# Scattering routed rows from the left and from the right: both choices sent without a wait between them

## The chip, the cores and the metric

One core of one Trainium2 chip runs the whole program in one launch. The metric is the device time of an execution in microseconds (us). PE is TensorE, DVE is VectorE, ACT is ScalarE, POOL is GpSimd, SP is SyncE, which here only issues DMAs. All data are float32.

## The reference, cut to what matters

Two layers run one after the other on x of 4 batches x 1024 rows x 256 columns (4096 rows, 32 tiles of 128 rows). The change is in the feed-forward part of the first layer:

```python
shared = silu(X @ sW1 + sb1) @ sW2 + sb2
logits = einsum('btd,ed->bte', X, routing_W) + expert_bias
activation = sqrt(softplus(logits))
top_vals, top_idx = top_k(activation, 2)          # 2 of 8 experts, with their weights
combine = sum(one_hot(top_idx, 8) * top_vals[..., None], axis=-2)
hdn = silu(einsum('nd,edh->enh', Xf, rW1) + rb1)  # h = 128
y = einsum('enh,ehd->end', hdn, rW2) + rb2
routed = einsum('ne,end->nd', combine, y)
x = x + shared + routed                            # X is layernorm(x)
```

Before it stands a memory update (a strided convolution over 64 rows and a layer norm, added to x); after it a second layer with cross attention to 64 context rows and a feed-forward part of 8 experts with its own routing.

## The kernel before, in words

Each engine has one instruction list written out by hand; semaphores order them. The first layer's feed-forward is done in two groups of 16 tiles (`LG = 2`, `LT = 16`). For group g:

- `memory_norm`, `memory_add` and `scores` (DVE) make the normed rows in the tile `N0`, PE turns them and makes the router's logits, ACT copies them out (`l_lt` counts these copies, `l_xa` those of the turned rows).
- `choose(g)` (DVE) picks the two best experts of each row, gives each (row, choice) a place in a list sorted by expert (`slots`), and the two weights. Weight 1 is written into the column behind the row in `N0`, weight 2 into `m2`. Then it raises `rout`.
- `send_rows(g)` (POOL) scatters each tile of 128 rows twice into the DRAM tensor `XS`, once for each choice, with an indirect DMA of whole rows of `XW = 260` elements: 256 of data, the weight, and padding. 16 DMAs go out for the first choice. Then, for each half of the tiles: wait until that half has landed, copy weight 2 over weight 1 in `N0` (L560), drain, and send the half for the second choice. In group 1 the sends are broken every four tiles by waits on `f_ys`, the count of routed tiles done.
- `routed_rows(g)` (SP) waits for all 32 scatters, and loads the list back in 40 tiles of 128 slots (`LS = 40`) into the buffers `fx`, six tiles ahead.
- `routed(g)`: DVE reads the tile's expert number into a register (`value_load`) and copies that expert's first matrix (`fw1`, L1706); PE transposes the tile (L863), DVE copies it out (`fxT`, L1708), PE makes the hidden layer, ACT applies silu, PE makes the output, and ACT scales it by the weight that came along in the row (`scale`, L1248). SP stores it to `YL`, from where POOL gathers it by row (L571). In PE's order iteration j is `xpose(j + 2)`, `up(j + 1)`, `down(j)`; DVE's `fw1` of tile j needs the silu of tile j - 2.

The order of the work around the change on PE and ACT is: `fold` of the attention weights for pairs 3 to 7 (ACT's copies are counted by `st_sb`), `shared_up` for group 0 (its silus are counted by `l_hs`), `scores(1)`, `shared_down` for group 0 (its copies are L1218, counted by `l_ev`), then `routed(0)`, the shared part of group 1, `routed(1)`, a meeting of all engines, and the second layer. `routed(0)` on PE waits for `l_ev` of all four quads; on DVE it follows `choose(1)`. The second layer's own sends (L621) already carry the weights on both sides of the row.

Of the kernel before, what the change touches and what calls it, by code (L numbers as in the profile page):

```python
# [89 lines left out]
def build(nc, x, ctx_in, conv_w, conv_b, rout_w, rout_b, sw1, sb1, sw2, sb2, rw1, rb1, rw2, rb2,  # L90
          wq, bq, wk, bk, wv, bv, wo, bo, wr, w1, w2, w3, out):
    st = ExitStack()
    with st:
# [61 lines left out]
        wcol = sb("wcol", [P, 4])  # L155
# [17 lines left out]
        N0 = sb("N0", [P, TILES, XW], stack=s1)  # L173
# [26 lines left out]
        fx = [sb(f"fx{k}", [P, XW], stack=s2)[:, :] for k in range(XB)]  # L200
# [29 lines left out]
        def row_tile(m):  # L230
# [46 lines left out]
            l_sa l_sb l_sc2 l_nr l_tp l_xa l_xd l_lg l_lt l_tn l_ev l_su l_hs l_sy l_xu  # L277
# [43 lines left out]
        def _(sp):  # L321
# [7 lines left out]
            def memory_rows(b):  # L329

                t0, k = b * BT, S // RATE
                sp.dma_start(N0[:, t0:t0 + 4, 0:D],
                             x[b, k:k + CONV, :].rearrange("(t p) d -> p t d", p=P)).then_inc(s[f"s_in{b}"], 16)
                sp.dma_start(N0[:, t0 + 4:t0 + 7, 0:D],
                             x[b, CONV + S:T - S, :].rearrange("(t p) d -> p t d", p=P)).then_inc(s[f"s_in{b}"], 16)
                sp.dma_start(N0[0:S, t0 + 7, 0:D], x[b, T - S:T, :]).then_inc(s[f"s_in{b}"], 16)
                sp.dma_start(N0[S:P, t0 + 7, 0:D], ctx_in[b]).then_inc(s[f"s_in{b}"], 16)

# [106 lines left out]
            for sent in ("l_sa", "l_sb"):  # L445
                sp.wait_ge(s[sent], 8 * LT * LG + 16 * FREED)
# [27 lines left out]
        def _(po):  # L474
# [38 lines left out]
            po.memset(N0[:, :, D:XW], 0.0)  # L513
# [25 lines left out]
            def send(k, t0, t1, done, slot0=None):  # L539

                for t in range(t0, t1):
                    if slot0 is not None and (t - t0) % BREAK == 0 and slot0 + SLOTS * ((t - t0) // BREAK) > 0:
                        po.wait_ge(s["f_ys"], slot0 + SLOTS * ((t - t0) // BREAK))
                    po.indirect_dma_start(  # L544
                        XS, bass.IndirectOffsetOnAxis(ap=slot[k][:, t:t + 1], axis=0),
                        N0[:, t, :], None).then_inc(s[done], 16)

            def send_rows(g):
# [3 lines left out]
                half = LT // 2  # L552
                parts = [(LT * g, "l_sa"), (LT * g + half, "l_sb")]
                step = SLOTS * half // BREAK
                paced = [step * i + 2 - SLOTS if g else None for i in range(4)]
# [60 lines left out]
            def scatter(k, t0, t1):  # L616

                part = (slice(0, X0 + D), slice(X0, XW))[k]
                for t in range(t0, t1):
                    done = ("l_sa", "l_sb")[k] if t < FREED else f"sc{k + 1}"  # L620
# [59 lines left out]
        def _(pe):  # L680
# [173 lines left out]
            def routed(g):  # L854
# [3 lines left out]
                def xpose(j):  # L858
# [3 lines left out]
                    for c in range(DC):  # L862
                        last = nc.tensor.transpose(bank[j % 2][:, c * P:c * P + P], fx[j % XB][:, c * P:c * P + P], ident[:, :])  # L863
# [239 lines left out]
        def _(ac):  # L1103
# [130 lines left out]
            def routed(g):  # L1234
# [9 lines left out]
                def scale(j):  # L1244
# [3 lines left out]
                    act(fy[j % YB], bank[(7, 5)[j % 2]][:, 0:D], ACT.Copy, scale=fx[j % XB][:, D:D + 1]).then_inc(s["f_ys"], 1)  # L1248
# [208 lines left out]
        def _(ve):  # L1457
# [121 lines left out]
            def memory_add(g):  # L1579

                k = P - S // RATE
                for b in (2 * g, 2 * g + 1):
                    ve.wait_ge(s[f"x_in{b}"], 16)
                    for i in (0, 1, 2, 4, 5, 6, 7, 3):
                        t, n = b * BT + i, {3: k, 7: S}.get(i, P)
                        stt(X[0:n, t, :], N0[0:n, t, 0:D], rstd[0:n, t:t + 1], X[0:n, t, :], ALU.mult, ALU.add)
# [624 lines left out]
```

## Time and profile before

| | |
|---|---|
| median of 3 runs | 910.0 us (909.23 to 913.66) |
| the profiled execution's own time | 908.59 us |
| its span | 906.8 us |
| PE, DVE, ACT, POOL busy | 87%, 55%, 54%, 47% of the span |
| mean granted TensorE clock | 0.952 of full speed |
| group 0's scatters on POOL | 89.15 to 144.70 us |
| first routed tile of group 0 on PE | 149.06 us |
| last matmul of group 1's routed tiles | 301.17 us |

Times within the span are counted from its start. The span is the time from the first to the last instruction of the profiled execution; the execution's own time is 1.8 us longer. An engine's idle time is put down to what ended it; "issue" means that the profile shows nothing that the engine waited for.

### The profile page before, as it was taken

How to read it: one execution, taken by the hardware profiler on the slowest of the kernel's cores; microseconds unless marked ns; L12 is line 12 of the kernel's file. 1: busy time of each engine (PE TensorE's matmuls, PEld its weight loads, DVE VectorE, ACT ScalarE, POOL GpSimd, SP SyncE). 2: the span in 40 equal slices, each digit the busy share in tenths (PEclk: the TensorE clock that was granted, in tenths of full speed). 3: DMA queues.
4: the chain of work that ended last, by engine and by line, in shares of the span. 5: the costliest groups of instructions: out<-in, count | busy, mean ns of one | idle time of the engine just before them, and what ended most of it. 6: DMA issues, size and time to landing. Idle time of an engine off the chain costs nothing.

```text
span 906.8 us, 16543 instructions
## 1 busy us (share of the span) xinstructions
PE 786.6 (87%) x4538; PEld 682.2 (75%) x4538; DVE 497.1 (55%) x1345; ACT 488.6 (54%) x1374; POOL 430.0 (47%) x398
## 2 busy tenths in 40 slices
PE   2989986888999689999999998784789999999992
PEld 1646545776778479999989997774689999999991
DVE  5837945532455468888889888670122222244242
ACT  1357644534466378888777785351334444445441
POOL 2200735552786079888546778246642222222221
PEclk9799997989999789999999998997999999999997
DMA  8899984765699693464600514622322222255524
GB/s 254 278 314 313 318 286 136 241 193 168 143 234 238 221 266 82 71 167 85 172 1 1 188 70 141 193 65 99 106 95 71 66 67 70 81 193 182 187 90 160
DMA packets 122115, 143.02 MB, mean 158 GB/s; under 512 B 10391, under 2 KB 113612, under 8 KB 121004
## 3 DMA queue, kind: packets, MB, share of 16 engines
q1 hardware_dynamic: 90520, 92.03, 33.8%
q0 software_dynamic: 19856, 38.88, 15.8%
q10 hardware_dynamic: 11654, 11.05, 3.7%
q8 instruction: 44, 0.72, 0.3%
q14 instruction: 41, 0.34, 0.1%
HBM read 71.28 MB, written 70.65 MB: 157 GB/s over the span
## 4 chain that ended last, share of the span: by engine, by line
PE 67%; issue 8%; DVE 6%; ACT 5%; POOL 4%; DMA 4%; another core or an unknown queue 3%; DVEq 1%; SPq 1%; POOLq 0%; ACTq 0%
PE psum L684 24%; PE psum L960 8%; PE psum L982 8%; PE psum L1048 5%; PE psum L1053 5%; PE psum L1049 5%; POOL xs_dram L544 3%; PE psum L970 3%; PE psum L1062 2%; ACT pr L1330 2%; PE psum L863 2%; PE psum L1032 2%; DMA X<-in_x_dram 1%; DMA fx<-xs_dram 1%
## 5 line engine op out<-in xcount | busy, mean ns | idle before, releaser
L633 POOL DMA_INDIRECT yk_dram<-ys,L x71 | 70.3, 990 | 201.3 <-ACT ys L1402 198.7
L1048 PE MATMUL psum<-whi,xTh 128*128 x284 | 110.4, 389 | 23.3 <-ACT xTh L1384 16.5
L2113 DVE TENSOR_TENSOR hs<-psum,hs 128x384 f32<-128x384 f32 x71 | 39.7, 559 | 151.0 <-PE psum L1053 102.9
L544 POOL DMA_INDIRECT xs_dram<-N,slots x64 | 66.8, 1043 | 108.0 <-DVEq L1687 50.8
L571 POOL DMA_INDIRECT X<-yl_dram,slots_y x64 | 100.5, 1571 | 35.4 <-issue 14.8
L1330 ACT ACTIVATE pr<-psum,nmx 128x64 f32<-128x64 f32 x512 | 108.0, 362 | 15.1 <-DVE nmx L2019 14.9
L684 PE MATMUL psum<-w_sb,cz 128*128 x426 | 104.5, 381 | 2.2 <-ACT ys L1402 1.2
L1049 PE MATMUL psum<-wlo,xTh 128*128 x284 | 96.9, 341 | 0.0
L684 PEld LDWEIGHTS psum<-w_sb,cz 128*128 128x128 f32 x426 | 75.8, 191 | 10.7 <-issue 3.3
L1053 PE MATMUL psum<-whi,xTl 128*128 x284 | 75.3, 346 | 3.9 <-DVE xTl L2132 3.9
L621 POOL DMA_INDIRECT xs_dram<-N,slots x64 | 66.6, 1040 | 21.4 <-issue 18.0
L1048 PEld LDWEIGHTS psum<-whi,xTh 128*128 128x128 f32 x284 | 54.7, 193 | 27.9 <-issue 26.3
L613 POOL TENSOR_TENSOR pr<-pr,sm 128x1024 f32<-128x1024 f32 x32 | 62.5, 1952 | 25.9 <-DVE sm L2026 23.2
L1390 ACT ACTIVATE cz<-psum 128x384 f32<-128x384 f32 x69 | 33.8, 490 | 74.6 <-PE psum L1062 52.0
L684 PE MATMUL psum<-rw_sb,fh 128*128 x160 | 55.9, 432 | 10.9 <-issue 5.4
L1396 ACT ACTIVATE hs<-psum 128x384 f32<-128x384 f32 x71 | 34.9, 492 | 54.6 <-PE psum L1053 44.3
L1402 ACT ACTIVATE ys<-psum,wcol 128x256 f32<-128x256 f32 x71 | 33.6, 473 | 45.0 <-PE psum L684 38.7
L1248 ACT ACTIVATE fy<-psum,fx 128x256 f32<-128x256 f32 x80 | 37.9, 473 | 34.1 <-PE psum L684 24.9
L1053 PEld LDWEIGHTS psum<-whi,xTl 128*128 128x128 f32 x284 | 52.2, 193 | 5.2 <-DVE xTl L2132 5.2
L1049 PEld LDWEIGHTS psum<-wlo,xTh 128*128 128x128 f32 x284 | 54.9, 193 | 1.6
L684 PE MATMUL psum<-fxT,fw 128*128 128x128 f32 x320 | 52.4, 289 | 4.0 <-DVE fxT L1708 1.9
L684 PE MATMUL psum<-b2p,ones 128*128 (+1 forms) x112 | 53.7, 479 | 0.0
(338 smaller groups left out, 1871.2 us busy)
## 6 DMA issues: line engine op xcount, KB each, us to landing
fx<-xs_dram SPq DMA_DIRECT2D x80, 130.0 KB
xs_dram<-fill SPq DMA_DIRECT2D x4, 2600.0 KB
yl_dram<-fy SPq DMA_DIRECT2D x80, 128.0 KB
xs<-xs_dram SPq DMA_DIRECT2D x71, 130.0 KB
wlo<-in_L_ffn_W_dram SPq DMA_DIRECT2D x4, 1536.0 KB, 7.0
ym<-yk_dram ACTq DMA_DIRECT2D x12, 512.0 KB
xs_dram<-cz SPq DMA_DIRECT2D x1, 5200.0 KB, 27.0
xs_dram<-cz SPq DMA_DIRECT2D x8, 650.0 KB
```

The lines of the kernel that those rows point to most:

```text
L544: po.indirect_dma_start(XS, bass.IndirectOffsetOnAxis(ap=slot[k][:, t:t + 1], axis=0), N0[:, t, :], None).then_inc(s[done], 16)
L571: po.indirect_dma_start(X[:, t, :], None, YL[b // 2], bass.IndirectOffsetOnAxis(ap=slot_y[k][:, t:t + 1], axis=0), compute_op=ALU.add).the ...
L613: po.tensor_tensor(v, v, sm[n % 2][:, :].rearrange("p (a b) -> p a b", b=1).to_broadcast([P, NHEAD, S]), ALU.mult).then_inc(s["a_pn"], 1)
L621: po.indirect_dma_start(XS1, bass.IndirectOffsetOnAxis(ap=slot[k][:, t:t + 1], axis=0), row_tile(t)[:, part], None).then_inc(s[done], 16)
L633: po.indirect_dma_start(YK, bass.IndirectOffsetOnAxis(ap=yid[:, j:j + 1], axis=0), ys[j % YB], None).then_inc(s[f"y_out{j % YB}"], 16)
L684: return nc.tensor.matmul(o, l, r, start=start, stop=stop)
L960: last = nc.tensor.matmul(bank[2 * b + h], a[b][:, c, :], w[k][:, c, cols_], start=i == c == 0, stop=i == 2 and c == DC - 1)
L982: last = nc.tensor.matmul(bank[7][:, 0:D], a[:, c * P:c * P + P], w[k][:, c, :], start=i == c == 0, stop=i == 2 and c == PAIRS - 1)
L1048: nc.tensor.matmul(o, xTh[b][:, c, :], wh[c], start=c == 0, stop=False)
L1049: nc.tensor.matmul(o, xTh[b][:, c, :], wl[c], start=False, stop=False)
L1053: last = nc.tensor.matmul(o, xTl[b][:, c, :], wh[c], start=False, stop=c == DC - 1)
L1330: last = act(pr[b][:, S * h:S * h + S], bank[2 * b + h // 8][:, S * (h % 8):S * (h % 8) + S], ACT.Exp, bias=nmx[:, h:h + 1])
```

## The change

- The row in `N0` is moved two elements to the right (`X0 = 2`): weight 1 stands in element 1, left of the data, and weight 2 in element 258, right of it. The first choice scatters elements 0 to 257, the second elements 2 to 259, into `XS` seen as single elements; `slots` therefore counts elements, in two `tensor_scalar` where there was one.
- With both weights in place, no row is rewritten between the choices. The waits for landing, the copies of weight 2 and the drains go.
- Where a choice doesn't write, the slot keeps the zero it was cleared to, so the weight of a slot is the sum of elements 1 and 258. DVE makes this sum for four tiles at a time into `wcol`, in each `j % 4 == 1`, with waits for the loads of the next two tiles and a drain behind it; ACT's `scale` reads `wcol` and waits for it in each `j % 4 == 0`.
- In group 0 the 32 scatters are broken by four waits: before number 8 for `st_sb`, 14 for `l_hs`, 20 for `l_xa`, 26 for `l_lt`. In group 1 the waits on `f_ys` stand at the same numbers as before.
- The semaphores `l_sa`, `l_sb`, `l_sc2` become `l_s0` and `l_s1`, one for each group.

```diff
-        wcol = sb("wcol", [P, 4])
+        wcol = sb("wcol", [P, XB])
...
-        N0 = sb("N0", [P, TILES, XW], stack=s1)
+        N0w = sb("N0", [P, TILES, XW], stack=s1)
+        N0 = N0w[:, :, X0:X0 + D]
...
-                for done in ("l_sa", "l_sb"):
-                    sp.wait_ge(s[done], 8 * LT * (g + 1))
-                sp.wait_ge(s["l_sc2"], 16 * LT * (g + 1))
+                sp.wait_ge(s[f"l_s{g}"], 16 * 2 * LT)
...
-            po.memset(N0[:, :, D:XW], 0.0)
+            po.memset(N0w[:, :, 0:X0], 0.0)
+            po.memset(N0w[:, :, X0 + D:XW], 0.0)
...
-                for (t, done), at_slot in zip(parts, paced):
-                    send(0, t, t + half, done, at_slot)
-                for (t, done), at_slot in zip(parts, paced[2:]):
-                    po.wait_ge(s[done], 16 * half * (g + 1))
-                    po.tensor_copy(N0[:, t:t + half, D:D + 1], m2[:, t:t + half].rearrange("p (t a) -> p t a", a=1))
-                    po.drain()
-                    send(1, t, t + half, "l_sc2", at_slot)
+                for i in range(2 * LT):
+                    k, t = i // LT, LT * g + i % LT
+                    if g and i and i % BREAK == 0:
+                        po.wait_ge(s["f_ys"], SLOTS * (i // BREAK) + 2 - SLOTS)
+                    if g == 0 and i == 8:
+                        po.wait_ge(s["st_sb"], 4 * PAIRS - 3)
+                    if g == 0 and i == 14:
+                        po.wait_ge(s["l_hs"], 2)
+                    if g == 0 and i == 20:
+                        po.wait_ge(s["l_xa"], LQ + 3)
+                    if g == 0 and i == 26:
+                        po.wait_ge(s["l_lt"], 2 * LQ)
+                    part = (slice(0, X0 + D), slice(X0, XW))[k]
+                    po.indirect_dma_start(
+                        XS1, bass.IndirectOffsetOnAxis(ap=slot[k][:, t:t + 1], axis=0),
+                        N0w[:, t, part], None).then_inc(s[f"l_s{g}"], 16)
...
-                    act(fy[j % YB], bank[(7, 5)[j % 2]][:, 0:D], ACT.Copy, scale=fx[j % XB][:, D:D + 1]).then_inc(s["f_ys"], 1)
+                    if j % 4 == 0:
+                        ac.wait_ge(s["f_xt"], j + 3)
+                    act(fy[j % YB], bank[(7, 5)[j % 2]][:, 0:D], ACT.Copy, scale=wcol[:, j % XB:j % XB + 1]).then_inc(s["f_ys"], 1)
...
-                ts(slots[:, :, t0:t0 + n], hot2[:, :, 0:n], float(base), None, ALU.add)
+                for k in range(2):
+                    ts(slots[:, k, t0:t0 + n], hot2[:, k, 0:n], float(XW), float(XW * base + X0 * k), ALU.mult, ALU.add)
...
-                tt(N0[:, t0:t0 + n, D], sp_x[:, 0, :], sp_r[:, 0, :], ALU.mult)
-                tt(m2[:, t0:t0 + n], sp_x[:, 1, :], sp_r[:, 1, :], ALU.mult)
+                tt(N0w[:, t0:t0 + n, X0 - 1], sp_x[:, 0, :], sp_r[:, 0, :], ALU.mult)
+                tt(N0w[:, t0:t0 + n, X0 + D], sp_x[:, 1, :], sp_r[:, 1, :], ALU.mult)
...
+                    if j % 4 == 1:
+                        k = j % XB - 1
+                        for i in (1, 2):
+                            ve.wait_ge(s[f"xs_in{(j + i) % XB}"], 16 * ((j + i) // XB + 1))
+                        if j > XB:
+                            ve.wait_ge(s["f_ys"], j - 5)
+                        tt(wcol[:, k:k + 4], fx8[:, k:k + 4, X0 - 1], fx8[:, k:k + 4, X0 + D], ALU.add)
+                        ve.drain()
```

## Rows read from the trace of the kernel before

**Rows 1.** The page's costliest groups; columns as in the page: busy, mean ns, idle before.

```profile
L544 POOL DMA_INDIRECT xs_dram<-N,slots x64 | 66.8, 1043 | 108.0 <-DVEq L1687 50.8
L621 POOL DMA_INDIRECT xs_dram<-N,slots x64 | 66.6, 1040 | 21.4 <-issue 18.0
```

**Rows 2.** The chain that ended last, 100 to 160 us: start, us, what.

```profile
111.51 6.75 issue
...
128.39 6.48 issue
...
143.74 2.25 DMA xs_dram<-N,slots
...
149.06 1.08 PE psum L863 x4
150.23 1.22 PE psum L684 x4
```

**Rows 3.** POOL in order of time: its DMAs and what follows a drain.

```profile
28.10 0.91 POOL L508 DMA_DIRECT2D wo_sb<-in_L_xattn_Wo_dram  x1
...
37.93 0.11 POOL L527 MEMSET segm<- 128x8 f32 x1 [5.93 <-issue]
...
128.17 0.21 POOL L560 COPY N<-m 128x8 f32<-128x8 f32 x1
```

**Rows 4.** The DMA issues: KB each, median us to landing.

```profile
wo_sb<-in_L_xattn_Wo_dram POOLq DMA_DIRECT2D x1, 1024.0 KB, 9.6
```

**Rows 5.** ACT in order of time, 100 to 145 us.

```profile
102.01 0.60 ACT L1175 ACTIVATE st_r<-psum 128x512 f32<-128x512 f32 x1 [0.26 <-issue]
...
108.98 0.69 ACT L1208 ACTIVATE cu<-psum,cols 128x512 f32<-128x512 f32 x1 [1.03 <-issue]
...
119.38 0.60 ACT L1191 ACTIVATE xT<-psum 128x512 f32<-128x512 f32 x1 [0.43 <-issue]
...
126.96 0.59 ACT L1185 ACTIVATE convw_sb<-psum 8x512 f32<-8x512 f32 x1 [2.01 <-PE psum L684]
...
141.92 1.08 ACT L1218 ACTIVATE ysh<-psum 128x512 f32<-128x512 f32 x2 [2.61 <-PE psum L684]
```

**Rows 6.** DVE in order of time: the end of choose(1) and the first routed tile.

```profile
140.36 0.18 DVE L1653 TENSOR_SCALAR slots<-hot 128x32 int32<-128x32 f32 x1
140.45 0.17 DVE L1654 CAST slots_y<-hot 128x32 int32<-128x32 f32 x1
...
144.28 0.40 DVE L1700 COPY rw_sb<-cols 128x8 f32<-128x8 f32 x1
145.75 0.31 DVE L1706 COPY fw<-rw_sb 128x257 f32 x1 [1.07 <-issue]
149.75 0.42 DVE L1708 COPY fxT<-psum 128x256 f32<-128x256 f32 x1 [3.69 <-issue]
```

**Rows 7.** DVE in order of time, one shared_add, one halt, a quick stretch.

```profile
164.96 1.22 DVE L1694 TENSOR_TENSOR X<-X,wq_sb 128x1024 f32<-128x1024 f32 x1
166.09 0.29 DVE L1706 COPY fw<-rw_sb 128x257 f32 x1
...
194.02 0.30 DVE L1706 COPY fw<-rw_sb 128x257 f32 x1 [2.94 <-issue]
...
199.94 0.42 DVE L1708 COPY fxT<-psum 128x256 f32<-128x256 f32 x1
200.90 0.30 DVE L1706 COPY fw<-rw_sb 128x257 f32 x1 [0.53 <-issue]
201.16 0.43 DVE L1708 COPY fxT<-psum 128x256 f32<-128x256 f32 x1
```

**Rows 8.** PE in order of time, the same quick stretch.

```profile
200.96 0.61 PE L684 MATMUL psum<-fxT,fw 128*128 128x128 f32 x4
...
202.18 0.61 PE L684 MATMUL psum<-fxT,fw 128*128 128x128 f32 x4
```

**Rows 9.** PE by windows of 2 us: busy (count), granted clock, DMA share, GB/s.

```profile
144.00:146.00 2.00, 0.00 (x0) 0.61 0.37 133
```

More of the change, by code:

```diff
@@ L199, in build @@
         sb("under_slots", [P, 2 * HK + TILES * XW + 3 * DC * NHEAD * DH], stack=s2)
-        fx = [sb(f"fx{k}", [P, XW], stack=s2)[:, :] for k in range(XB)]
+        fx8 = sb("fx8", [P, XB, XW], stack=s2)
+        fx = [fx8[:, k, :] for k in range(XB)]
         fxT = [sb(f"fxT{k}", [P, DC, P], stack=s2)[:, :, :] for k in range(2)]
@@ L331, in memory_rows @@
                 t0, k = b * BT, S // RATE
-                sp.dma_start(N0[:, t0:t0 + 4, 0:D],
+                sp.dma_start(N0[:, t0:t0 + 4, :],
                              x[b, k:k + CONV, :].rearrange("(t p) d -> p t d", p=P)).then_inc(s[f"s_in{b}"], 16)
-                sp.dma_start(N0[:, t0 + 4:t0 + 7, 0:D],
+                sp.dma_start(N0[:, t0 + 4:t0 + 7, :],
                              x[b, CONV + S:T - S, :].rearrange("(t p) d -> p t d", p=P)).then_inc(s[f"s_in{b}"], 16)
-                sp.dma_start(N0[0:S, t0 + 7, 0:D], x[b, T - S:T, :]).then_inc(s[f"s_in{b}"], 16)
-                sp.dma_start(N0[S:P, t0 + 7, 0:D], ctx_in[b]).then_inc(s[f"s_in{b}"], 16)
+                sp.dma_start(N0[0:S, t0 + 7, :], x[b, T - S:T, :]).then_inc(s[f"s_in{b}"], 16)
+                sp.dma_start(N0[S:P, t0 + 7, :], ctx_in[b]).then_inc(s[f"s_in{b}"], 16)
             def x_rows(b):
@@ L443, in _ @@
             weights(2)
-            for sent in ("l_sa", "l_sb"):
-                sp.wait_ge(s[sent], 8 * LT * LG + 16 * FREED)
+            sp.wait_ge(s["l_s1"], 16 * 2 * (LT + FREED))
             weights(3)
@@ L537, in after @@
                     po.wait_ge(s[other], n)
[L539 to L546, printed above, removed]
             def send_rows(g):
@@ L551, in send_rows @@
                 po.wait_ge(s["rout"], g + 1)
[L552 to L555, printed above, removed]
-                for (t, done), at_slot in zip(parts, paced):
-                    send(0, t, t + half, done, at_slot)
-                for (t, done), at_slot in zip(parts, paced[2:]):
-                    po.wait_ge(s[done], 16 * half * (g + 1))
-                    po.tensor_copy(N0[:, t:t + half, D:D + 1], m2[:, t:t + half].rearrange("p (t a) -> p t a", a=1))
-                    po.drain()
-                    send(1, t, t + half, "l_sc2", at_slot)
+                for i in range(2 * LT):
[14 more added lines that the diff above has]
+                        N0w[:, t, part], None).then_inc(s[f"l_s{g}"], 16)
             def collect(b, k, t0, t1):
@@ L619, in scatter @@
                 for t in range(t0, t1):
-                    done = ("l_sa", "l_sb")[k] if t < FREED else f"sc{k + 1}"
+                    done = "l_s1" if t < FREED else f"sc{k + 1}"
                     po.indirect_dma_start(
@@ L862, in xpose @@
                     for c in range(DC):
-                        last = nc.tensor.transpose(bank[j % 2][:, c * P:c * P + P], fx[j % XB][:, c * P:c * P + P], ident[:, :])
+                        last = nc.tensor.transpose(bank[j % 2][:, c * P:c * P + P], fx[j % XB][:, X0 + c * P:X0 + c * P + P], ident[:, :])
                     last.then_inc(s["f_tp"], 1)
@@ L1601, in rows_in @@
                     for t in range(QT * q, QT * q + QT):
-                        last = ts(N0[:, t, 0:D], X[:, t, :], mean[:, t:t + 1], rstd[:, t:t + 1], ALU.subtract, ALU.mult)
+                        last = ts(N0[:, t, :], X[:, t, :], mean[:, t:t + 1], rstd[:, t:t + 1], ALU.subtract, ALU.mult)
                     last.then_inc(s["l_nr"], 1)
```

6 lines of the change are left out of this document (3 added, 3 removed).

## The prediction

> **What bounds the kernel now.** I read the page first: PE is busy 87% of the span, so most of the program is PE work, and POOL's scatter L544 appears high among the groups with 64 instructions and 66.8 us [rows 1]. A share of the span doesn't say whether a scatter costs time, so I went to the chain of work that ended last and looked at 100 to 160 us. There the chain isn't on PE: it runs through group 0's scatters on POOL, through two gaps of 6.75 and 6.48 us before the 17th and the 25th scatter, then a landing of 2.25 us, the load of a tile, and only then PE's first routed tile at 149.06 and its first hidden layer at 150.23 [rows 2]. That is the stretch that the change touches. To see what would be late next I read ACT, DVE and PE in order of time around it [rows 5 to 8], and the granted clock there [rows 9].
>
> **What the two gaps are.** Each gap stands behind a copy of weight 2 (the second copy at 128.17 [rows 3]), not before it, so when the copy ran the half that it rewrites had landed, and what took 6.5 us was the drain. POOL's other drain behind DMAs looks the same: the last weight load is issued at 28.10, takes 9.6 us to land [rows 4], which is 37.7, and POOL goes on at 37.93 after 5.93 us of idle time [rows 3]. So a drain on POOL seems to last until what POOL has sent has landed. The change removes the copies (0.2 us each) and these drains: 6.75 + 6.48 + 0.4 = 13.6 us off POOL's own line.
>
> **What the four waits give back.** One scatter follows another by 1.27 us (0.96 us and 0.30 us of issue, the pitch in the undisturbed runs of them). The eighth started at 100.13.
> - Number 8 (counted from 0) would start at 101.4; it waits for the copy that ACT starts at 102.01 and ends at 102.61 [rows 5], and with 0.3 us of release starts at 102.9.
> - Number 14 would start six pitches later, 110.5; its silu ended at 109.67 [rows 5], so it waits for nothing.
> - Number 20: 118.1, but the turned rows that it waits for are out at 119.98 [rows 5], so 120.3.
> - Number 26: 127.9; the logits that it waits for are out at 127.55 [rows 5], nothing.
> - Number 31, the last: 127.9 + 5 x 1.27 = 134.2, against 143.74 before.
>
> So the scatters end 9.5 us sooner; 4 us of the 13.6 go to the waits. The loads would be there 9.5 us sooner too, which puts PE's first transpose at 139.5 as far as data go.
>
> **What is late next.** PE can't start `routed(0)` before ACT's last shared copy, which ends at 143.0 [rows 5]; that is still no limit, because DVE comes later. It has `choose(1)` to finish, then the bias copy at 144.28, and `fw1` of the first tile at 145.75 [rows 6]. In the kernel before `fw1` was already there and `fxT` waited for the tile until 149.75. After the change the tile waits for DVE. Where nothing holds it up, `fxT` starts 0.26 us behind `fw1` (200.90 and 201.16 [rows 7]). To this come the split `slots` instruction: the start-to-start step of such a small one is 0.09 us [rows 6], once in each `choose`, both on DVE's line to this point, 0.18 us. So `fxT` starts at 145.75 + 0.18 + 0.26 = 146.19 instead of 149.75. **The gain at the start of routed(0) is 3.6 us, not 9.5 and not 13.6.** This line has a cushion for the scatters: their landing may take up to 142.4 (146.2 less the 3.1 us from landing, 145.99, to the first transpose, and the 0.7 us from there to `fxT` [rows 2, 6]), 7 us after the last one is issued. Landing took 2.25 us when the DMA engines had little to do [rows 2], about 6.5 us in the busier time behind each drain. Both fit. If the cushion were used up, each us over it is a us of the gain.
>
> **What the weight sums cost.** There are 20 of them, with a drain each, on DVE. The trace has no such operation; it has two neighbours. One is the bias copy, also with a drain behind it and a register load next: `fw1` starts 1.07 us after the copy's end [rows 6]. Applied to a sum of 0.17 us that starts 0.34 us behind the start of `fxT`, it puts the next `fw1` 1.58 us behind `fxT`. In the quick stretch it starts 0.96 us behind (199.94 to 200.90), and the next `fxT` 0.26 us after it [rows 7]. That is 0.62 us later for DVE. The low end is 0.11 us: 0.59 us until the drain is through, and 0.48 us for the register load (no less than 0.56 us from `fxT` start to `fw1` start is seen anywhere, less the step of issue). PE needs the copy that started at 201.16 only for the hidden layer at 202.18, and the copy ends at 201.59 [rows 7, 8]: 0.6 us of slack. The other neighbour is `shared_add`: it occupies DVE for 1.22 us and `fw1` starts 1.13 us after it, 1.48 us behind `fxT` [rows 7], and PE's period around it isn't visibly longer than elsewhere in this stage, while the quick stretch has 1.22 us [rows 8]. With 0.62 us more against 0.6 us of slack and 0.1 us from the copy's end to PE's start, one sum costs between 0 and 0.12 us of PE's time in the quick stretch, and nothing in the slower ones. I take 0.05 us, as the sums lie nearest to `shared_add`: 20 x 0.05 = 1.0 us, bounds 0 and 20 x 0.12 = 2.4 us. Without PE's slack it would be 20 x 0.62 = 12.4 us.
>
> The DVE row says that a drain with a register load behind it has a price of 1.07 us [rows 6]. The Trainium skill ("VectorE: DVE Perf Modes", section "The DRAIN you can't avoid") says that every DVE instruction has its pipeline flush anyway and that adding synchronization costs nothing extra. By that the drains would be free, the sums only 0.17 us each, and the total for them 0 instead of 1.0 us. Only the instruction behind it is counted there, not a register load; the row here is the dearer one and the sum goes by it.
>
> **Costed at nothing.** ACT's wait in `j % 4 == 0` needs `fxT` of tile j + 2. That copy follows its transposes, which PE does before `up(j + 1)` and `down(j)`; in the quick stretch it ends 0.5 us before the output that ACT scales is made, 0 if the sum takes the full 0.62 us; silu of the next tile stands behind it and has a tile of slack. DVE's waits for the loads of the next two tiles: the loads run six tiles ahead, and PE waits for tile j + 2 before `up(j + 1)` anyway; behind DVE's wait stand `fw1` and `fxT`, which PE wants at the same moment. Scaling by `wcol` instead of `fx`: the same instruction. The second memset of POOL stands before the drain that waits for a landing until 37.9 [rows 3], so its 0.15 us is covered; uncovered it would be just that. Scatter of 258 instead of 260 elements: the second layer's L621 does this at 1040 ns against 1043 ns [rows 1]. Group 1's scatters: their copies and drains go too, but the last batch still hangs on `f_ys` 32, and POOL isn't on the chain there. Its first four stay where they are, behind `rout` at about 144.4.
>
> **The sum.** -3.6 + 1.0 = -2.6 us. The span goes from 906.8 to 904.2 and the profiled execution's own time from 908.59 to 906.0. The median of the runs shown was 910.0, 1.4 us above that execution, so I forecast 907.4. From `routed(0)` on everything hangs on PE and moves along with it: POOL's gathers start on the stores of group 0, the meeting of the engines on the last tile of group 1.
>
> **Rivals.**
> - *More comes back than the start.* PE stood idle from 142 to 149, its granted clock fell (0.61 in the mean of 144 to 146 [rows 9]) to the lower of its two levels, 1.2 GHz. Now four transposes can run at 143.1, and PE is idle for 3 us instead of 7. The first hidden layer took 1.22 us there and takes 0.61 us at the full clock [rows 2, 8]. If the clock stays up, the first two save 0.6 us each, 1.2 us together, and the rest of those tiles stands beside other waits. The Trainium skill ("TensorE: Matmul & The Clock Gate", Part 1) has the lower level as the default and activity as what lifts it; by that rule the transposes may or may not do, so it gives 906.2 or 907.4. Also, in `routed(0)` the engines stood still before 194.02, DVE for 2.94 us with nothing to wait for [rows 7], just after POOL had sent eight scatters without a break, the first four of them late by the drain. If spreading them cures this: 907.4 - 2.9 = 904.5, and with both 903.3. Against: nothing in the profile ties the halt to the scatters. Chance 0.27.
> - *The weight sums are not covered.* Slower than before: DVE's 0.62 us shows on PE at each of 20 places, 910.0 - 3.6 + 12.4 = 918.8. It eats the gain from 0.18 us for each sum on, and is slower by over 0.5% from 0.41 us on. For it: the DVE line of `fw1`, `fxT`, `up`, silu is a loop of its own, near PE's pace. Against: `shared_add` of 1.22 us leaves no such mark. Chance 0.12.
> - *The scatters land late.* Their last six now go out at 128 to 135, while the expert weights are loaded. If landing takes 10 us or more, the start hardly moves: 910.0 - 0.5 + 1.0 = 910.5. Chance 0.08.
> - *The whole shift of 9.5 us counts.* Only if `choose(1)` came earlier too, which nothing in the change does: 901.5. Chance 0.03.
> - My forecast, 905.2 to 909.2: 0.50.
>
> **How the numbers follow.** 0.5% is 4.55 us, about what a measurement of this kernel can tell from no change; faster means under 905.45, slower over 914.55. Faster: 0.8 of the first rival (0.22), the fourth (0.03), and 0.07 of my own case: 0.32. Slower: most of the second rival, 0.10. The same: 0.58. The range reaches to the first rival's 903.3 less 0.8 us and up past the third's 910.5 by the top of the sums' bound: 902.5 to 912. Left out are the fourth rival, the dear end of the second and the tails.
>
> **What the profile after would show.** Right: no gap over 3 us in POOL's group 0 scatters except 1.3 us before number 8 and 2 us before number 20; the last one starts near 134; `fx` loads near 138; PE transposes two tiles near 143.2, then waits for DVE; the first `fxT` at about 146.2. The period of PE in `routed(0)` and `routed(1)` unchanged outside the halts, 20 additions of under 0.2 us. Wrong: `fxT` of the first tile waits for a load, or `routed(1)` ends less than 2 us earlier than 301.2 with the start 3.6 us earlier (the sums cost), or the halts of `routed(0)` are shorter or longer by more than 2 us, which would outweigh both terms.

## The result and the profile after

The changed kernel takes 928.81 us (median of 4 runs, 926.69 to 929.46) against 909.62 us (4 runs): ratio 1.0222 [1.0178, 1.0265]. It is slower by 2.2%, well clear of the noise. (Ratios compare executions in the chip's fast state alone, medians are of all executions, so the two need not divide exactly.) The forecast was 907.4 us with a range up to 912. The profiled execution has a span of 924.9 us, 18.1 us longer than before's.

The page's groups for the two sends, to compare with [rows 1]: a scatter is as quick as before, and POOL's idle time ahead of the first layer's went up from 108.0 to 125.2 us.

```profile
L556 POOL DMA_INDIRECT xs_dram<-N,slots x64 | 64.4, 1006 | 125.2 <-DVEq L1686 68.7
...
L617 POOL DMA_INDIRECT xs_dram<-N,slots x64 | 65.8, 1029 | 21.3 <-issue 18.0
```

I followed the same stretch first: the chain of work that ended last, 84 to 165 us. Columns as in [rows 2].

```profile
113.02 7.48 another core or an unknown queue
120.52 0.70 DVE xT L1607
...
134.53 10.20 another core or an unknown queue
144.75 1.09 ACT wq_sb L1214 x2
...
161.82 0.23 DVE fxT L1707
162.09 0.71 PE psum L680 x4
```

The scatters and the two gaps of [rows 2] are off the chain, as forecast. In their place stand two pieces of 7.48 and 10.20 us for which the profile names no instruction. The first routed tile's hidden layer starts at 162.09 instead of 150.23 [rows 2]. The same two places, engine by engine in order of time (POOL's first four rows; then DVE, ACT, PE):

```profile
98.26 1.28 POOL L556 DMA_INDIRECT xs_dram<-N,slots  x1 [0.31 <-issue]
103.33 0.97 POOL L556 DMA_INDIRECT xs_dram<-N,slots  x1 [3.79 <-ACT st_r L1171]
...
117.34 0.97 POOL L556 DMA_INDIRECT xs_dram<-N,slots  x1 [0.30 <-issue]
127.67 0.96 POOL L556 DMA_INDIRECT xs_dram<-N,slots  x1 [9.36 <-ACT xT L1187]
...
141.75 0.97 POOL L556 DMA_INDIRECT xs_dram<-N,slots  x1 [0.30 <-issue]
```

```profile
120.52 0.69 DVE L1607 COPY xT<-psum 128x512 f32<-128x512 f32 x1 [7.50 <-remote]
```

```profile
120.52 1.08 ACT L1187 ACTIVATE xT<-psum 128x512 f32<-128x512 f32 x2 [5.54 <-remote]
144.75 1.08 ACT L1214 ACTIVATE wq_sb<-psum 128x512 f32<-128x512 f32 x2 [10.22 <-remote]
```

```profile
121.36 3.57 PE L680 MATMUL psum<-xT,cols 128*8 128x512 f32 x4 [5.87 <-DVE xT L1607]
145.98 1.19 PE L680 MATMUL psum<-sw_sb,cu 128*128 128x256 f32 x2 [8.60 <-ACT wq_sb L1214]
```

"Remote" means that the engine started when a semaphore rose, but that the profile found no instruction ending close enough to have raised it. I call such a place a halt.

The trace's record of semaphores tells whose signal it was: PE's. At the first place both engines wait for the semaphore of the transposes of L776, at the second ACT waits for that of the shared output matmuls. PE in order of time, and DVE's last instruction of its part of `choose(1)`:

```profile
113.52 1.97 PE L776 MATMUL psum<-ident,N 128*128 128x128 f32 x16 [0.78 <-issue]
...
136.91 0.47 PE L680 MATMUL psum<-b2p,ones 128*128 128x256 f32 x1
```

```profile
140.20 0.19 DVE L1674 TENSOR_TENSOR sp_x<-sp_x,m 128x32 f32<-128x32 f32 x1
```

The transposes are recorded as ended at 115.49 (113.52 + 1.97), and their semaphore rises at 120.50, 5.0 us later. The matmuls end at 137.38 (136.91 + 0.47), and theirs rises at 144.73, 7.35 us later. ACT and DVE start 0.02 us behind the rise each time, the same PE rows as in e4 are there without a gap, and DVE works on inside the second halt until 140.39. So a halt is a late signal of PE's, and part of the idle time in front of it (2.5 of DVE's 7.5 us, 2.85 of ACT's 10.2 us) is an ordinary wait for PE's work. Whether the matmuls themselves finished late (the profile models the ends of PE's work) or only their signals came late, the trace doesn't tell.

Now to when the signals come. POOL's scatters 8 to 19 end at 118.31 (117.34 + 0.97), and DVE and ACT come back 2.21 us later. Scatters 20 to 31 end at 142.72, and ACT comes back 2.03 us later. Of the four waits, two break nothing: numbers 14 and 26 follow without a gap, so POOL issues 12 scatters in a row, twice.

The stage behind it is longer as well. Times of `fxT`, first tile to last of each group (`routed(0)` is tiles 0 to 39, `routed(1)` 40 to 79), from DVE in order of time:

| | first scatter to first fxT | routed(0) | routed(1) | last fxT to the end |
|---|---|---|---|---|
| before | 60.6 | 69.3 | 58.8 | 608.4 |
| after | 73.0 | 69.3 | 64.9 | 608.3 |

So 12.4 us are lost ahead of the first routed tile and 6.1 us in `routed(1)`, and nothing elsewhere: 18.5 us, and the span is 18.1 us longer. In `routed(1)` each `fxT` after a weight sum comes late: the mean step from tile j to j + 1 is 2.66 us for j % 4 == 1, against 1.64 us before; the other three steps together are 0.4 us shorter. One such place, DVE, ACT, PE, SP in order of time:

```profile
266.58 0.43 SPq L398 DMA_DIRECT2D fx<-xs_dram  x1
...
271.57 0.42 DVE L1707 COPY fxT<-psum 128x256 f32<-128x256 f32 x1
...
272.01 0.37 ACT L1238 ACTIVATE fh<-psum,fw 128x128 f32<-128x128 f32 x1 [0.19 <-PE psum L680]
...
273.14 0.17 DVE L1714 TENSOR_TENSOR wcol<-fx 128x4 f32<-128x4 f32 x1 [1.15 <-DMA fx<-xs_dram]
...
273.78 0.38 PE L859 MATMUL psum<-ident,fx 128*128 128x128 f32 x2
274.28 0.30 DVE L1705 COPY fw<-rw_sb 128x257 f32 x1 [0.98 <-ACT fh L1238]
274.49 0.42 DVE L1707 COPY fxT<-psum 128x256 f32<-128x256 f32 x1
274.96 0.71 PE L680 MATMUL psum<-fxT,fw 128*128 128x128 f32 x4 [0.80 <-DVE fxT L1707]
275.02 0.47 ACT L1246 ACTIVATE fy<-psum,wcol 128x256 f32<-128x256 f32 x1 [1.26 <-DVE fxT L1707]
```

This is tile 53. DVE wants the load of tile 55, which SP had issued at 266.58 (counted by the stores between), and waits 1.15 us for it. PE transposes tile 55 only at 273.78, so the load came in time for PE. Then come the sum, the drain and the register load, and `fw1` of tile 54 starts 1.14 us after the sum. Its silu had ended at 272.38 (272.01 + 0.37); the wait put down to it was long over. PE idles 0.80 us and ACT 1.26 us. And since ACT's `scale` now waits for `fxT`, the count `f_ys` by which SP loads further tiles is held up too.

### The profile page after: what moved, and what is told of

The parts are those of the page before. It is cut to its first block, busy times and chain, and to the rows that moved or that the text cites. A ratio compares the mean times of both kernels' runs of the same rounds, so it can differ in the third digit from the quotient of the medians.

```text
span 924.9 us, 16596 instructions
## 1 busy us (share of the span) xinstructions
PE 789.5 (85%) x4538; PEld 681.1 (74%) x4538; DVE 500.4 (54%) x1367; ACT 487.8 (53%) x1374; POOL 423.6 (46%) x395
## 4 chain that ended last, share of the span: by engine, by line
PE 56%; DVE 11%; issue 8%; another core or an unknown queue 5%; POOL 5%; DMA 5%; ACT 4%; DVEq 4%; SPq 2%; POOLq 0%; ACTq 0%
PE psum L680 21%; PE psum L956 6%; PE psum L1044 5%; PE psum L978 5%; PE psum L1049 5%; PE psum L1045 5%; DMA fx<-xs_dram 3%; PE psum L1058 2%; POOL xs_dram L617 2%; PE psum L966 2%; PE psum L1028 2%; POOL pr L609 2%; ACT pr L1328 1%; DMA X<-in_x_dram 1%
## 5 line engine op out<-in xcount | busy, mean ns | idle before, releaser
L629 POOL DMA_INDIRECT yk_dram<-ys,L x71 | 69.5, 979 | 202.2 <-ACT ys L1400 200.4
L556 POOL DMA_INDIRECT xs_dram<-N,slots x64 | 64.4, 1006 | 125.2 <-DVEq L1686 68.7
L567 POOL DMA_INDIRECT X<-yl_dram,slots_y x64 | 100.0, 1563 | 33.6 <-issue 14.8
L1328 ACT ACTIVATE pr<-psum,nmx 128x64 f32<-128x64 f32 x512 | 108.0, 362 | 11.8 <-DVE nmx L2026 11.5
L617 POOL DMA_INDIRECT xs_dram<-N,slots x64 | 65.8, 1029 | 21.3 <-issue 18.0
L680 PE MATMUL psum<-fxT,fw 128*128 128x128 f32 x320 | 52.3, 288 | 10.1 <-DVE fxT L1707 8.6
L1246 ACT ACTIVATE fy<-psum,wcol 128x256 f32<-128x256 f32 x80 | 37.8, 473 | 40.4 <-PE psum L680 21.3
```

The costliest lines, as they stand in the source:

```text
L556: po.indirect_dma_start(XS1, bass.IndirectOffsetOnAxis(ap=slot[k][:, t:t + 1], axis=0), N0w[:, t, part], None).then_inc(s[f"l_s{g}"], 16)
L567: po.indirect_dma_start(X[:, t, :], None, YL[b // 2], bass.IndirectOffsetOnAxis(ap=slot_y[k][:, t:t + 1], axis=0), compute_op=ALU.add).the ...
L617: po.indirect_dma_start(XS1, bass.IndirectOffsetOnAxis(ap=slot[k][:, t:t + 1], axis=0), row_tile(t)[:, part], None).then_inc(s[done], 16)
L629: po.indirect_dma_start(YK, bass.IndirectOffsetOnAxis(ap=yid[:, j:j + 1], axis=0), ys[j % YB], None).then_inc(s[f"y_out{j % YB}"], 16)
L680: return nc.tensor.matmul(o, l, r, start=start, stop=stop)
L1328: last = act(pr[b][:, S * h:S * h + S], bank[2 * b + h // 8][:, S * (h % 8):S * (h % 8) + S], ACT.Exp, bias=nmx[:, h:h + 1])
```

## The experiments

Theory A: the engines halt because their next instructions don't come while POOL issues scatters without a pause; the drains before were the pauses. (What PE's late signals say of theory A stands under "What ends a halt".) Theory B: the weight sums cost the time. Theory C: the bulk transfers (expert weights, clearing) halt the engines whatever POOL does. Each call ran on one chip, with the kernel before beside it, and the chips turned out to differ: the kernel before takes 902 to 910 us on some and 866 to 868 us on others. Ratios are therefore always to before on the same chip.

**First call: group 0's breaks (before 867.62 us).** The four waits are replaced by before's drains, by nothing, or by short memsets; e4 keeps them and breaks group 1's scatters at every second one.

```diff
 e1_drains:   if g == 0 and i in (16, 24): po.drain()
 e2_one_run:  (nothing)
 e3_gaps:     if g == 0 and i and i % 4 == 0: three po.memset(scratch), each with a semaphore
 e4_pairs:    if g and i >= 4 and i % 2 == 0:
                  po.wait_ge(s["f_ys"], SLOTS * i // BREAK + 2 - SLOTS)
```

> The changed kernel with the four waits of group 0 replaced by a POOL drain before scatters 16 and 24; the weights stay on both sides, the weight sums stay. Theory A (an engine that needs its next instructions gets them only when POOL pauses between scatters, and the two halts of 7.5 and 10.2 us come from two unbroken runs of 12): the drains pause POOL for 6 to 7 us near 110 and 127 as in the kernel before, no halt over 3 us in 100 to 150 us, time 905 to 912. Rival B (the weight sums and their waits cost the 19 us): nothing changes there, 926 to 931. Rival C (the halts come from bulk transfers that fill the DMA engines, whatever POOL does): halts stay, 920 to 930.

> The changed kernel with no wait at all within group 0's 32 scatters: one run from 88.6 to about 129.3. Theory A: ACT and DVE, who want instructions near 113, halt until 1.5 to 2.2 us after the run's end, 131; then nothing is in the way of choose(1); first routed tile at 159 to 162, 920 to 930. Rival B: the scatters end earlier, 926 to 931 all the same, but without a halt at 131. Rival C: halts of the same length as in the changed kernel at about the same times, 926 to 931.

> The changed kernel with the four waits replaced by a short pause of POOL before every fourth scatter of group 0: three small memsets, each waited for by its semaphore (about 1 to 1.5 us). Theory A, if a pause of 1 us is enough: no run longer than 4 scatters, halts under 4 us, time 902 to 910. If the pause must be longer: one run until about 138, 930 to 940. Rival B: 926 to 931. Rival C: 920 to 931.

> The changed kernel with group 1's scatters broken after every second one instead of every fourth (waits on f_ys at even numbers, same average pace); group 0 as it is. Theory A: the two halts of group 0 stay, the halts in routed(0) (ends at 198.4, 209.1, 219.5, 228.2) shrink by 1 to 2 us each, 920 to 926. Rivals B and C: as the changed kernel, 926 to 931.

Measured: e1 882.05 us, 1.0171 [1.0108, 1.0233]; e2 874.89, 1.0095 [1.0056, 1.0133]; e3 871.67, 1.0054 [1.0023, 1.0085]; e4 873.71, 1.0069 [1.0039, 1.0098]. Theory A had the drains among the best; they are the worst. None of the four traces has a single halt, not even e2 with 32 scatters in a row. On this chip theory A has nothing to explain, and yet all four are slower than before. What they share is the weight sums.

**Second call: the sums (before 907.88 us).** e5 and e6 are the two kernels unchanged. e7 leaves the sums out, so that the rows of the second choice get weight 0; e8 makes them one tile at a time behind `fxT`, of a tile that has been transposed and so is there:

```diff
-                    if j % 4 == 1:
-                        ... (waits for two loads and f_ys)
-                        tt(wcol[:, k:k + 4], fx8[:, k:k + 4, X0 - 1], fx8[:, k:k + 4, X0 + D], ALU.add)
-                        ve.drain()
+                    tt(wcol[:, j % XB:j % XB + 1], fx[j % XB][:, X0 - 1:X0], fx[j % XB][:, X0 + D:X0 + D + 1], ALU.add).then_inc(s["f_w"], 1)
...
-                    if j % 4 == 0:
-                        ac.wait_ge(s["f_xt"], j + 3)
+                    ac.wait_ge(s["f_w"], j + 1)
```

> The kernel before, unchanged, so that its trace is there from the same chip as the others. Theory A (the engines halt while POOL scatters in long runs): its routed(0) takes longer than routed(1) by the halts, as in the first trace (69.3 us against 58.8 us from the first to the last fxT). Theory B (the weight sums cost the time): whatever the halts do, routed(1) takes 58 to 59 us, and the kernels with sums take about 6 us longer there (64 to 66 us).

> The changed kernel, unchanged. Theory A: ratio to before 1.015 to 1.03 wherever the halts show in the trace, and near 1.00 where they don't. Theory B: 10 to 13 us for the 20 sums, less 3 to 9 us that the start of routed(0) gains: ratio 1.003 to 1.01 without halts, and routed(1) 6 us longer than before's.

> The changed kernel without the 20 weight sums, their waits and their drains; ACT scales by the element on the left alone, so the second choice's rows get weight 0 (that part of the computation is left out). Theory B: 10 to 13 us under the changed kernel on the same chip, ratio to before 0.990 or less, routed(1) at 58 to 59 us. Theory A: the same time as the changed kernel within 3 us. My prediction's term: 1.0 us (0 to 2.4).

> The changed kernel with the weight summed tile by tile on DVE, right behind fxT, with a semaphore of its own and with neither a drain nor a wait for the loads of later tiles. Theory B in the form that the drain and the wait for loads cost the time, not the addition: within 3 us of the kernel without sums, ratio to before about 0.99. If the addition itself costs it: 80 x 0.15 us = 12 us over the kernel without sums. Theory A: no difference to the changed kernel.

Measured: e5 912.32 us in its one execution. e6 922.57, 1.0205 [1.0143, 1.0267]. e7 913.42, 1.0117 [1.0057, 1.0177]. e8 912.97, 1.0107 [1.0045, 1.0169]. The sums as the change makes them cost 9.2 us here (922.57 - 913.42, six executions each); made tile by tile, 80 additions in place of 20, they cost nothing measurable. So it isn't the addition (0.15 us each, in DVE's idle time) but what stands around it. With the sums gone the kernel is still slower than before by 1.2% [0.6%, 1.8%], and the stretch ahead of the first routed tile, with its halts, is what is left to differ (70.3 us against 60.2 in e5). They stand in e6, e7 and e8 at the same two places as in the first trace. e6, ACT in order of time:

```profile
117.97 1.08 ACT L1187 ACTIVATE xT<-psum 128x512 f32<-128x512 f32 x2 [5.29 <-remote]
...
141.38 1.08 ACT L1214 ACTIVATE wq_sb<-psum 128x512 f32<-128x512 f32 x2 [10.21 <-remote]
```

**Third call: the sums tile by tile, and group 0 in four ways (before 868.37 us).** e9 has the drains of e1, e10 the gaps of e3, e12 one run as e2, and e11 twelve memsets (3 us) before each of scatters 8, 16 and 24. All have e8's sums.

> Weights summed tile by tile, and in group 0 two drains on POOL (before scatters 16 and 24, where the kernel before has them) instead of the four waits. Theory A: where the halts exist, the stretch from the first scatter to the first fxT is that of the kernel before, 60 to 61 us, instead of 70 to 73 us; together with free sums the ratio to before is 0.995 to 1.003. Theory C (the DMA engines are full, whatever POOL does): the stretch stays at 70 us and the ratio at 1.01. On a chip without halts the drains keep the stretch at 61 us instead of 54 us: ratio 1.00.

> Weights summed tile by tile; group 0 in runs of four scatters with 0.8 us of memsets between them, instead of the four waits. Theory A: if 0.8 us lets a refill through, the halts are at most 5 us each, the stretch to the first fxT is 56 to 62 us, ratio 0.99 to 1.00; if a pause has to be longer than the 1.5 to 2.2 us by which the engines come back after a run, it is 70 us or more, as with one run. Theory C: 70 us. Without halts: 54 us, ratio 0.992.

> Weights summed tile by tile; group 0 in four runs of eight scatters with 3 us of memsets between them, instead of the four waits. Theory A: pauses are longer than the time in which the engines come back, so the halts shrink to what is left of a run: stretch 56 to 62 us, ratio 0.99 to 1.00. Theory C: 70 us, 1.01. Without halts: 54 us, ratio 0.992.

> Weights summed tile by tile; group 0's 32 scatters in one run of 41 us with no pause. Theory A: an engine that runs out of instructions behind the first scatters stands until 1.5 to 2.2 us after the run, so one halt of 15 to 19 us that ends 43 to 44 us after the first scatter, and the first fxT about 74 us after it; ratio 1.01 to 1.015. Theory C: halts at the same times as in the changed kernel, whether POOL's run goes on or not. Without halts: 54 us, ratio 0.992.

Measured: e9 868.03 us, 1.0007 [0.9977, 1.0037]; e10 863.23, 0.9939 [0.9915, 0.9962]; e11 862.66, 0.9940 [0.9907, 0.9973]; e12 862.25, 0.9939 [0.9915, 0.9963]. Again no halts, so A and C stay untested. But the parts come out clean. With the drains kept, the new layout of the rows costs and brings nothing (e9 = before). Taking the drains away brings 5.8 us (e9 to e12). How POOL is paced makes no difference. e12, DVE in order of time at the end of `choose(1)`:

```profile
142.07 0.17 DVE L1690 COPY rw_sb<-cols 128x8 f32<-128x8 f32 x1
143.32 0.49 DVE L1696 COPY fw<-rw_sb 128x257 f32 x1 [1.08 <-issue]
143.73 0.40 DVE L1698 COPY fxT<-psum 128x256 f32<-128x256 f32 x1
```

The tile is there, and `fxT` follows `fw1` by 0.41 us: DVE's own line sets the start, as forecast. With one run POOL's first scatter starts at 89.52 and `fxT` 54.21 us later. It is 54.20 to 54.22 us in all eight traces without halts of kernels that have neither drains nor pauses of 3 us, e4 with its four waits included; with the 3 us pauses it is 55.7 to 56.1 us.

**Further draws of a chip.** The kernels of e12 and e11 again, to meet a chip with halts; at last the changed kernel once more. (e13 to e16 ran on one and the same chip.)

> The same kernel as the one with one run of 32 scatters, for a chip on which the halts exist (before at about 909 us). Theory A: a halt of 15 to 19 us that ends 1.5 to 2.2 us after the run (43 to 44 us after the first scatter), first fxT about 74 us after the first scatter, ratio 1.01 to 1.015. Theory C: halts of 6 to 7 us and 10 us at the places of the changed kernel, 70 us. On a chip without halts (before at about 868 us): 54 us, ratio 0.994, as measured.

> The same kernel as the one with four runs of eight scatters and 3 us of memsets between them, for a chip on which the halts exist. Theory A: halts end within the pauses, so none is longer than 7 us and they sum to less than in the changed kernel: first fxT 56 to 62 us after the first scatter, ratio 0.99 to 1.00. Theory C: 70 us, 1.01. Without halts: 54 to 56 us, 0.994.

> One run of 32 scatters, weights tile by tile, in search of a chip on which the halts exist. Theory A there: first fxT about 74 us after the first scatter, the last halt ending 43 to 44 us after it, ratio 1.01 to 1.015. Theory C: 70 us, the halts at the places of the changed kernel. Without halts: 54 us, 0.991 to 0.994.

> Four runs of eight with 3 us of memsets between them, weights tile by tile, same chip as the run of 32. Theory A where halts exist: first fxT 56 to 62 us after the first scatter, ratio 0.99 to 1.00, no halt over 7 us. Theory C: 70 us, 1.01. Without halts: 54 to 56 us, 0.994 to 0.996.

> One run of 32 scatters, weights tile by tile, a further draw of a chip. Theory A where halts exist: the last halt ends 43 to 44 us after the first scatter and the first fxT is about 74 us after it. Theory C: first fxT at 70 us, halts where the changed kernel has them, the first ending 32 us after the first scatter. Without halts: 54 us, ratio 0.991 to 0.995.

> The changed kernel, unchanged, on a further draw of a chip. If the halts don't exist there (before at about 867 us), the stretch from the first scatter to the first fxT is 54 to 55 us as in the kernels with one run, and the sums cost 11 to 13 us over the kernels that sum tile by tile (which stand at 0.991 to 0.997): ratio 1.005 to 1.010. If they exist (before at about 908 us), the stretch is 70 to 73 us and the ratio 1.015 to 1.025, as on the two chips before. The theory that the halts alone make the change slow expects 0.99 on a chip without them.

Measured: one run 0.9914 [0.9881, 0.9947], 0.9949 [0.9913, 0.9985] and 0.9932 [0.9883, 0.9980] (e13, e15, e17); runs of eight 0.9964 [0.9929, 1.0] and 0.9976 [0.9928, 1.0024] (e14, e16), before at 865.7 to 867.9 us each time and no halts. Only e18 met a chip with halts, with the wrong kernel for the question: 922.44 us against 902.35, 1.0210 [1.0174, 1.0246]. It repeats the first result, with halts of 6.35 and 10.18 us.

**What separates the chips.** Times in us; the halts are those of over 1.3 us put down to "remote" ahead of the first routed tile:

| kernel (before on its chip) | halts | first scatter to first fxT | first to last fxT | last fxT to the end |
|---|---|---|---|---|
| before, first trace (909.6) | 6.5 | 60.6 | 148.7 | 608.4 |
| e5, before (907.9) | 2.3, 1.5, 4.1 | 60.2 | 147.9 | 609.0 |
| after, first trace (909.6) | 7.5, 10.2 | 73.0 | 155.0 | 608.3 |
| e6, after (907.9) | 6.4, 10.2 | 70.5 | 153.5 | 608.2 |
| e18, after (902.4) | 6.4, 10.2 | 69.9 | 150.5 | 609.2 |
| e7, no sums (907.9) | 6.7, 10.1 | 70.3 | 145.4 | 607.6 |
| e8, sums by tile (907.9) | 6.4, 9.4 | 71.5 | 142.9 | 607.3 |
| e1, drains (867.6) | none | 61.5 | 148.3 | 581.0 |
| e9, drains, by tile (868.4) | none | 60.3 | 135.9 | 581.2 |
| e2, one run (867.6) | none | 54.2 | 145.2 | 580.9 |
| e12, one run, by tile (868.4) | none | 54.2 | 136.1 | 579.5 |

The last column belongs to code that the change doesn't touch, and differs by 27 us between the chips. Most of it is the end of the stretch in which POOL sends the second layer's scatters and those behind them (L617 and L629): from 290 to 380 us behind the last `fxT` PE idles 24.3 us in after and 3.1 us in e12, and 66.7 against 43.3 us in the whole column. PE by windows, after and then e12: busy (count), other engines, granted clock, DMA share, GB/s.

```profile
600.00:700.00 100.00, 75.37 (x399) 69.11 (x398) 33.50 (x127) 35.09 (x90) 51.42 (x57) 0.90 0.27 88
```

```profile
600.00:700.00 100.00, 100.00 (x582) 95.16 (x581) 26.88 (x77) 48.33 (x128) 48.81 (x51) 1.00 0.34 103
```

In after DVE stands in that stretch for up to 12.8 us with "remote"; in e12 no engine does. The DMA share is 0.27 and 0.34: no shortage of DMA engines.

**What ends a halt.** In the five traces with the change's waits and with halts, POOL's second run of scatters ends between 115.90 and 122.48 us and the third between 139.35 and 145.50; the engines come back behind them by:

| | after | e6 | e7 | e8 | e18 |
|---|---|---|---|---|---|
| behind scatter 19 | 2.21 | 2.07 | 2.03 | 2.02 | 2.00 |
| behind scatter 31 | 2.03 | 2.03 | 1.94 | 1.21 | 1.99 |

In the first trace of before, where the run ends elsewhere, DVE's halt of 6.54 us ends at 129.82, 1.64 us behind the end of its run of eight (128.18). Against it stands one halt of e5, 2.27 us, that ended at 110.80 inside a run that went on to 114.66. So ends of long halts follow ends of POOL's runs, closely; that the one causes the other was not tested, as the kernels with longer and with shorter runs met no chip with halts.

The semaphores of all 20 traces carry it further. In the 13 traces without halts no signal of PE's, of some 890 in each, rises more than 0.015 us behind the recorded end of the work that raises it. In the seven with halts 245 rise over 1 us behind it. All of these lie inside a run of three or more of POOL's scatters (in the second layer also those of the outputs, L629) or at most 2.7 us behind one. None lies beside the 64 gathers (L567), which are indirect DMAs as well. The longest delay grows with the length of the run, by and large: 3.3 us for runs of four scatters, 6.1 us for eight, 7.35 us for twelve and 13.1 us for fourteen, but only 2.0 us for before's run of sixteen. This speaks for the half of theory A that ties the halts to runs of scatters. Counting in traces isn't an experiment, though: the runs differ in other ways too, and where a matmul's record is missing a single delay is less than it seems.

Against theory C: the second halt of after lies in 134.5 to 144.8, where the DMA share is 0.33 in both windows that hold it, on the same core that shows 1.02 in 88 to 98 us without a halt over 1.3 us. These are `after`'s windows:

```profile
88.00:98.00 10.00, 10.00 (x40) 7.43 (x40) 8.77 (x35) 7.08 (x14) 7.51 (x7) 1.00 1.02 325
...
132.00:142.00 10.00, 5.04 (x26) 2.89 (x25) 4.38 (x15) 0.97 (x2) 7.57 (x9) 0.91 0.33 116
142.00:146.00 4.00, 0.02 (x1) 0.05 (x1) 0.00 (x0) 1.08 (x2) 0.72 (x1) 0.50 0.33 110
```

The other half of theory A is that a halted engine is out of instructions. The page of after lists two queues for instructions:

```profile
q8 instruction: 44, 0.72, 0.3%
q14 instruction: 41, 0.34, 0.1%
```

The Trainium skill ("Runtime: NRT & Kernel Launch", section "Instruction fetch mechanics") says that instructions are fetched in blocks of 16 KiB over a DMA queue of their own, and that this is mostly hidden. For q8 the size agrees (0.72 MB in 44 packets), q14's packets are half as large. That a late fetch makes the halts is what the trace speaks against. ACT and DVE weren't out of instructions, as they started 0.02 us behind PE's signal. And the second halt goes by without a fetch: these are all the queues that moved anything in after from 123 to 152 us, and none is one for instructions.

```profile
q1 hardware_dynamic: 3749, 3.81, 41.4%
q0 software_dynamic: 576, 1.59, 15.2%
```

The second halts of e6, e7, e8 and e18 have no such packet either. Inside the first halt of after one packet starts, at 115.55, and it is over at 116.49, 4.0 us before the signal. What holds PE's signals back stays open.

## Why the prediction was wrong

- **The two gaps are drains that wait for landing: right.** With drains in place of the waits the gaps are back at their places (9.04 and 6.62 us in e1, 8.26 and 6.32 us in e9, against 6.75 and 6.48 us [rows 2]).
- **The four waits give back 4 us, last scatter at 134.2: wrong, and without weight where there are no halts.** Number 20 went at 127.67 instead of 120.3, as the turned rows that it waits for came out behind the first halt. In e4, without halts, scatter 31 starts 43.8 us after the first (forecast 134.2 - 89.15 = 45.05) and the start of `routed(0)` is that of one run.
- **The gain at the start, 3.6 us: this step failed.** Its mechanism is right (DVE's `choose(1)` and `fw1` come last; 54.21 us in e12), and without halts it brings 6.1 us (e9 to e12, 60.27 to 54.21). But the term took DVE's line from the trace before as fixed: `fxT` at 146.19, 57.0 us behind the first scatter. That line hangs on PE's signals. Without late ones it takes 54.2 us, so those of the trace before had put 2.8 us into it. In the changed kernel it takes 73.0 us, and e4, with the same group 0 on a chip without halts, 54.2: the halts cost 18.8 us there, and the start came 11.9 us later instead of 3.6 us earlier. Before had halts as well and lost nothing by them at the start (60.6 and 60.2 us with halts, 60.3 us in e9 with drains and without halts), because POOL's line with its drains ended last and covered them. The change took the cover away, and the halts grew: ahead of the first tile the longest delay of a signal is 1.8 and 2.0 us in the two traces of before and 7.35 us in after. That the cover is gone and that they grew is shown by these numbers, why they grew isn't. I had seen one halt [rows 7], and counted its cure as a possible gain, with the remark that nothing tied it to the scatters. The mirror of it, that the change makes them longer, stands in the prediction only as a sign of being wrong, for `routed(0)`, and was no rival with a price.
- **The weight sums, 1.0 us (0 to 2.4): this step failed too.** They cost 9.2 us by the medians of e6 and e7, and 9 to 12 us between e2 and e12 or e1 and e9 by the time from the first to the last `fxT` (145.2 to 136.1, 148.3 to 135.9). The second rival had this at 12.4 us, with a chance of 0.12. Two entries under "costed at nothing" were wrong. "The loads run six tiles ahead": they are issued six tiles ahead, but for tile 55 it took 6.5 us from the issue to the start of the sum, and DVE, whose line is ahead of PE's, asks for them earlier than PE does; it idled for them 11 times, 13.6 us, in e1. And ACT's wait for `fxT` of tile j + 2 had slack only as long as that copy isn't late: it waited 7.8 us in seven places (150 to 300 us of after). How much is the drain with the register load and how much the early wait wasn't separated: e8 takes both away. The low price rested on a gap of 1.58 us from `fxT` to the next `fw1`. At tile 53 it was 2.71 us (271.57 to 274.28), as the wait for the load came on top. (That no step from `fxT` to `fw1` is under 0.56 us doesn't hold either: one is 0.33 us in the trace before, 242.26 to 242.59. The figure went only into the low end.)
- **The slack of 0.6 us on PE [rows 7, 8] and `shared_add` as a neighbour** were the reason for the low price. The slack is real in a quick stretch, but the sum doesn't come there: it waits for loads, which `shared_add` doesn't.
- **The sum.** -3.6 + 1.0 should have been, for the first chip, +12.4 ahead of the first tile (the stretch counted from the first scatter, which went out 0.5 us earlier) and +6.1 in `routed(1)`. In `routed(0)` the sums disappear beside the halts of that stage (69.3 us before and after; 65.9 with and 65.7 without sums in e6 and e7).
- **The other rivals.** Scatters that land late: no, `fxT` waited for no load at the start. The whole shift of 9.5 us: no. The clock: its lower level did not go away but spread. The granted clock is 0.50 in 142 to 146 us of after, 1.2 GHz, where PE had done nothing since 137.38.

The version that sums tile by tile and sends group 0 in one run beats both kernels where there are no halts (0.9914 to 0.9949 in four comparisons on three chips). What it does where there are, is open; of the kernels measured there, the kernel before is the fastest.

## What to carry to other kernels

A wait for data ahead of need isn't free because the data are "issued far ahead": compare the issue-to-landing time with the lead in us, at the engine that runs first. Reduce what has been waited for already, in small pieces with a semaphore of its own, before batching it with a drain. And idle time that a trace puts down to nothing in the program is no constant: look up when the awaited semaphore rose and when the work that raises it had ended, and price its growth as a rival of its own when the change moves it or lays it bare.

## What the hardware showed that I had not expected

- The same kernel takes 866 to 868 us on some chips and 902 to 910 us on others (medians of before in eight comparisons; the chip of the first result is of the second kind). The difference goes with late signals of PE's: a semaphore rises up to 13.1 us behind the recorded end of the matmul that raises it, at a DMA share of 1.0 and of 0.3 alike, where otherwise 0.015 us is the most. No trace from a chip of the first kind shows one over that, though all 13 are of changed kernels, with up to 32 scatters in a row.
- The late signals keep to runs of POOL's scatters and the 2.7 us behind them, and avoid its gathers. The two long halts end 1.2 to 2.2 us behind the end of the run in 10 of 10 cases with the changed kernel's waits.
- A drain on POOL behind scatters stands for 6.3 to 9.0 us; one of DVE with a register load behind it puts the next copy at least 0.95 us behind the start of the sum (1.14 us at tile 53).
